# What GpSimd waits for before its indirect transfers: landings, or TensorE's counts

## The reference, cut to what matters

```python
# x: (8, 512, 256) f32; 32 experts, 6 of them per token
xn = layernorm(x)
s = attention_over_channels(xn)         # per batch: softmax over a 256x256 matrix of channels
for e in range(32):                     # combine: softmax gate, 3 of 8 groups, top 6, normalized
    y += combine[:, e] * ((silu(xn @ w1[e].T) * (xn @ w3[e].T)) @ w2[e].T)
shared = (silu(xn @ sw1.T) * (xn @ sw3.T)) @ sw2.T
out = x + s * silu(y + shared)
```

## Time and profile before

| | |
|---|---|
| median of 3 runs | 969.05 us (965.66 to 969.32) |
| profiled execution, its own time | 964.12 us |
| its span | 962.4 us |
| PE / DVE / POOL / ACT busy | 596.8 / 506.7 / 399.2 / 341.5 us |
| mean granted clock of PE | 0.804 |
| DMA moved | 174.75 MB, mean 182 GB/s |

### The profile page before, as it was taken

How to read it: one execution, slowest core, us unless ns; L and a number is a source line. 1 busy time by engine, 2 the same in 40 slices (tenths; PEclk the granted TensorE clock), 3 DMA queues, 4 the chain that set the end, 5 groups by cost and what they waited for, 6 DMA issues and landing times.

```text
span 962.4 us, 13698 instructions
## 1 busy us (share of the span) xinstructions
PE 596.8 (62%) x3728; PEld 486.4 (51%) x3728; DVE 506.7 (53%) x1412; ACT 341.5 (35%) x684; POOL 399.2 (41%) x401
## 2 busy tenths in 40 slices
PE   5788782928375776001979776758486765658540
PEld 4567551817164654001968665546375654547430
DVE  7877863736374771000535555546465645646543
ACT  3343431332323242001646443435254443435330
POOL 0135345455364663663001444343444444453443
PEclk9798795867768686655979797879799897979875
DMA  9994572634524223224437675758677675848552
GB/s 335 390 356 164 182 262 93 234 132 140 210 73 141 76 93 132 82 82 136 145 120 218 192 237 171 219 154 251 176 220 224 189 208 168 241 148 259 164 170 76
DMA packets 134232, 174.75 MB, mean 182 GB/s; under 512 B 12433, under 2 KB 120722, under 8 KB 133266
## 3 DMA queue, kind: packets, MB, share of 16 engines
q1 hardware_dynamic: 109698, 107.77, 34.3%
q0 software_dynamic: 18432, 50.36, 17.4%
q10 hardware_dynamic: 6032, 15.76, 4.7%
HBM read 81.56 MB, written 92.28 MB: 181 GB/s over the span
## 4 chain that ended last, share of the span: by engine, by line
DMA 57%; issue 21%; POOL 9%; PE 8%; DVE 4%; POOLq 1%; ACT 0%; SPq 0%; DVEq 0%; ACTq 0%
DMA early<-slots_d,slot_at 30%; DMA slots_d<-early,slot_at 23%; POOL slots_d L391 7%; PE ps L696 4%; DMA slots_d<-pad 3%; DVE ps L957 3%; POOL early L408 2%; PE ps L715 2%; PE ps L684 1%; PE ps L706 1%; DVE work L974 1%; POOLq L391 0%; SPq L290 0%; DMA work<-slots_d 0%; DMA slots_d<-early 0%
## 5 line engine op out<-in xcount | busy, mean ns | idle before, releaser
L408 POOL DMA_INDIRECT early<-slots_d,slot_at x192 | 191.7, 999 | 316.9 <-DVE ps L957 108.2
L391 POOL DMA_INDIRECT slots_d<-early,slot_at x192 | 205.4, 1070 | 237.8 <-DMA slots_d<-early,slot_at 170.5
L696 PE MATMUL ps<-w_all,work 128*128 x1344 | 186.5, 294 | 57.3 <-issue 54.2
L696 PEld LDWEIGHTS ps<-w_all,work 128*128 128x128 f16 x1344 | 140.5, 105 | 83.1 <-issue 60.4
L684 PE MATMUL ps<-ident,work 128*128 128x128 f32 x448 | 75.2, 294 | 140.1 <-DMA work<-slots_d 65.9
L957 DVE SCALAR_TENSOR_TENSOR ps<-early,wk,ps 128x256 f32<-128x256 f32 x160 | 77.8, 486 | 116.9 <-DMA early<-slots_d,slot_at 115.5
L684 PEld LDWEIGHTS ps<-ident,work 128*128 128x128 f32 x448 | 54.7, 151 | 155.7 <-issue 81.4
L974 DVE SCALAR_TENSOR_TENSOR work<-ps,work 128x512 f16<-128x512 f32 x112 | 76.8, 686 | 103.6 <-ACT work L517 102.1
L517 ACT ACTIVATE work<-ps 128x512 f16<-128x512 f32 x112 | 66.6, 595 | 141.0 <-PE ps L684 128.1
L715 PE MATMUL ps<-w_all,work 128*128 x672 | 99.9, 289 | 2.5 <-DVE work L987 2.0
L524 ACT ACTIVATE work<-ps 128x256 f32<-128x256 f32 x112 | 43.0, 384 | 157.1 <-PE ps L696 127.4
(11 more groups left out here) (140 smaller groups left out, 811.6 us busy)
## 6 DMA issues: line engine op xcount, KB each, us to landing
work<-slots_d SPq DMA_DIRECT2D x112, 256.0 KB
slots_d<-early SPq DMA_DIRECT2D x112, 256.0 KB
slots_d<-pad SPq DMA_DIRECT2D x7, 3072.0 KB, 15.5
w_all<-in_wexp ACTq DMA_DIRECT2D x7, 1536.0 KB, 6.9
slots_d<-pad SPq DMA_DIRECT2D x1, 7168.0 KB, 30.0
s_all<-in_x SPq DMA_DIRECT2D x8, 512.0 KB, 4.8
ysh_d<-work ACTq DMA_DIRECT2D x8, 512.0 KB
early<-ysh_d SPq DMA_DIRECT2D x32, 128.0 KB
```

Source lines behind the costliest of these rows:

```text
L391: pool.indirect_dma_start(slots_d[:, :], bass.IndirectOffsetOnAxis(ap=slot_at[:, at:at + 1], axis=0), xn[b % XN_RING][:, t, :], None, boun ...
L408: pool.indirect_dma_start(gath[:, at % RING, :], None, slots_d[:, :], bass.IndirectOffsetOnAxis(ap=slot_at[:, at:at + 1], axis=0), bounds_ ...
L696: mm = pe.matmul(ps[:, 2 + p % 2, h * 2 * I:(h + 1) * 2 * I], xT[p % 2][:, x_low, h, k, :], w16[:, bass.ds(at_weights[2 * p + h] + w_low * ...
```

## The change

GpSimd no longer waits for the landing of its own transfers. In stage 1 every second scatter waits for a count that PE raises: the function `let_pass` gives for scatter n of batch b the semaphore and the value, in the order in which PE reaches them, from the turn of batch b+1 to the first product of batch b+1's attention. The last batch has six such waits, the last of them for PE's last count of the stage. In stage 2 a gather of pair q (two per pair) waits for PE's hidden matmuls of pair q+21 if it is even, and for PE's transposes of pair q+20 if it is odd, both capped at the last pair; the waits for stores and for the ring stay. The scatters' semaphores are three now, one per `xn` buffer, and all who wait for scatters wait on these. SP waits for batches 2 and 5 alone before it loads the last weights.

```diff
-FLIGHT = 2
@@ semaphores
-        s_disp = sems("s_disp", FLIGHT)
+        s_disp = sems("s_disp", XN_RING)
@@ SP
-            for f in range(FLIGHT):
-                sp.wait_ge(s_disp[f], 16 * (BATCH_ROWS // FLIGHT) * (B - 2))
+            sp.wait_ge(s_disp[2], 16 * BATCH_ROWS * 2)
...
-            for f in range(FLIGHT):
-                sp.wait_ge(s_disp[f], 16 * (BATCH_ROWS // FLIGHT) * B)
+            for k, n in enumerate((3, 3, 2)):
+                sp.wait_ge(s_disp[k], 16 * BATCH_ROWS * n)
@@ GpSimd
+            def let_pass(b, n):
+
+                nxt = b + 1 < B
+                due = {4: (s_s_ps, b + 1), 8: (s_y_ps, 2 * b + 1), 10: (s_r_ps, b + 1), 12: (s_y_ps, 2 * b + 2),
+                       14: (s_m_ps, b + 1), 18: (s_at_ps, 2 * b + 2)}
+                if nxt:
+                    due.update({2: (s_xt_ps, 2 * b + 4), 6: (s_lg_ps, b + 2), 16: (s_cnt, b + 2),
+                                20: (s_ab_ps, HC * b + HC + 1), 22: (s_a_ps, b + 2)})
+                if n in due:
+                    pool.wait_ge(*due[n])
+
...
-                        if at >= FLIGHT:
-                            pool.wait_ge(s_disp[at % FLIGHT], 16 * (at // FLIGHT))
+                        let_pass(b, t * TOP_K + k)
...
-                                                oob_is_err=False).then_inc(s_disp[at % FLIGHT], 16)
+                                                oob_is_err=False).then_inc(s_disp[b % XN_RING], 16)
...
-                    if at >= FLIGHT:
-                        pool.wait_ge(s_gath[(at - FLIGHT) % RING], 16 * ((at - FLIGHT) // RING) + 16)
+                    ahead = at // 2 + 21
+                    if at % 2 == 0:
+                        pool.wait_ge(s_eab_ps, min(ahead + 1, PAIRS))
+                    else:
+                        pool.wait_ge(s_ehT_ps, min(ahead, PAIRS))
@@ DVE, normal(b)
-                    for f in range(FLIGHT):
-                        dve.wait_ge(s_disp[f], 16 * (BATCH_ROWS // FLIGHT) * (b - XN_RING + 1))
+                    dve.wait_ge(s_disp[b % XN_RING], 16 * BATCH_ROWS * (b // XN_RING))
```

## The result

The changed kernel takes **813.48 us** (median of 4 executions, 805.62 to 827.74), the kernel before beside it 967.99. Two of the four executions (819.64 and 827.74) fell in a slower state and are left out of the ratio, which is 0.8333, 95% interval 0.8299 to 0.8368; the other two took 805.62 and 807.32. The forecast was 765 with a range of 745 to 820. The profiled execution took 805.62 us for a span of 803.8. Of the 158.6 us by which the span fell, 117.2 came before the expert stage starts; the rest came in that stage, 473.3 us long where it had been 514.7, and forecast were 434.5.

The account below looks back on a forecast made before the run. Bound by latency of GpSimd's indirect DMA transfers and waits for their landing, not traffic. Terms 327.1 + 87.7 + 311.5 + 35.3 = 761.6 span, 763.3 for the execution, 766 with run offset, stated as 765; range 745 to 820.

Parts of the forecast that it names:

- Rival 1: Stage 2: store and gather each land 3 us later, using up the slack; a dozen takes 48.4, total 792; chance 0.17.
- Rival 2: Both stages: indirect transfers are served one after the other, 1.59 us per scatter; stage 2 +64, 829; chance 0.12.
- Rival 4: Stage 1 keeps half its wait because GpSimd, released in bursts, falls behind; 795 us; chance 0.06.
- (a): Stage 1: scatters released by TensorE's counts end line 755's landing wait, batches every 37.57 us; 60.9 us saved.
- (b): End of stage 1: the last expert weights wait for batch 5 alone and come 5.6 us earlier.
- (c): Scatter tail after TensorE's stage 1 work: stage 2 starts at 327.1 instead of 447.67, 120.6 us earlier in all.
- Start to pair 24: Beginning of stage 2, from its first slot load to pair 24: as before, 87.7 us.
- (d): Stage 2: gathers released by TensorE's counts, dozens of 43.4 us; seven 311.5 with 1.1 each for crowded DMA, 63.8 saved.
- (e): End of stage 2, from pair 108 on: 35.3 us instead of 51.75, 16.4 saved.
- the slack of 4.9 us: Stage 2: sum 0's gathers and sums need 17.5 us of the 22.4 between pair 18 and pair 26.
- Rival 3: Stage 2 release loop: gathers wait on TensorE, TensorE on sums, sums on gathers; slower, 970 and more; chance 0.03.
- my 315: Stage 2: DMA engines move 315 GB/s at most, 2.9 us per pair, adding up to 1.1 us a dozen.

Follow-up runs that it names:

- g1: The kernel before with the change's gathers only, scatters still waiting for landings; 86.0 us saved, stage 2 takes 429.0 us.
- c1: The changed kernel without the scatters' waits for TensorE's counts (`let_pass` left out); a batch takes 44.0 us, total not given.
- f3: b1 with a waited write of 1024 columns on GpSimd after every second gather; 820 us.
- b1: The changed kernel with its gathers waiting for no count of TensorE, only for the ring's free place and the stores; 858 us.
- d1: The changed kernel with each gather fetching 64 of 256 columns, a quarter of the bytes; a dozen takes 49.3 us, total not given.

## Why the prediction was right, and what it missed

The sign and the two mechanisms held. The size held with luck: 813.48 lies in the range of 745 to 820, but outside the forecast's own 748 to 785, and in it only by the room made for rivals 1, 2 and 4, none of which was what happened. The profiled span was forecast at 761.6 and is 803.8; term by term, 42.2 us:

- **(a), (b), (c), stage 1: 3.4 us short.** The period is 37.5 as forecast, and the landing waits at the refill went. Scatters had fallen behind their counts at the end: the last 15 ran back to back, and the last started at 327.96, against 324.6 forecast (6.5 and 2.5 make 326.9 and not the 327.1 that I wrote; the landing in that row is 2.55). Rival 4 (half of the wait kept) fell. On chips I and II it would have been 12 to 16 us short; "remote" waits stand in stage 1 there, and in this profile too (line 490, 37.7 us).
- **Start to pair 24:** 87.2, forecast 87.7.
- **(d), the dozens: the term that failed, 36.1 of the 42.2.** "The sums stop waiting" held: 7.4 us left. "So a dozen costs 43.4" didn't follow here, because I took it that a count is there when TensorE is done, and it was late 55 times. Where counts aren't late, it does follow: g1 has dozens of 43.5, with the register loads bare (7.7 and 8.4 us of idle time at two of them) as I had put it, and the whole stage takes 429.0 where I had 434.5. The 1.1 us that I added for crowded queues weren't needed.
- **(e), the tail:** 38.5 instead of 35.3; g1 has 36.7.
- The median lies 7.9 above the profiled execution, where I had allowed 2. The four executions spread over 22 us; the twelve kernels of the experiments spread over 1 to 12, with and without late counts, so what set the two long ones apart isn't known.

**The rivals.** Rival 1 came nearest in the length of a dozen (48.4, and 49.6 measured), for the wrong reason: the sums hardly wait for a landing, so the slack of 4.9 us held. Rival 2 fell: transfers overlap, 15 scatters went out at 1.28 us each to the end and the last landed within 2.6 us of its start. Rival 3, the loop, would show as sums waiting for gathers, and doesn't. What the list lacked was a cost of the burst itself: before, runs of gathers are of one or two, and I read their harmlessness as a property of the transfers and not of the spacing.

**Where DMA could bind.** g1's stretches, with two columns at the end, DMA share and GB/s:

```profile
721.00:726.00 5.00, 4.86 (x45) 4.25 (x43) 4.44 (x11) 3.32 (x8) 2.17 (x3) 1.00 1.00 321
726.00:731.00 5.00, 4.85 (x45) 4.22 (x43) 4.77 (x12) 3.60 (x8) 2.99 (x3) 1.00 0.99 298
```

The engines are full at 321 GB/s, near my 315 and short of the 358 that the Trainium skill, DMA: Bandwidth & Descriptors, Specifications, gives. TensorE's pairs go on meanwhile: from 716.31 to 742.23 nine take 2.88 us each, 0.26 over the quiet 2.62. So full queues can have cost 2.6 us a dozen at most, with VectorE's sums in the same 0.26.

**Do the parts add up?** The scatters alone saved 105.5 us (chip I), the gathers alone 86.0 (chip III), both together 161.5 by the two executions of the ratio (154.5 by the median). The 30 us between are near what the dozens lost in the changed kernel (36.1) and g1's did not, but the three figures come from different chips, and stage 1 alone differs by some 10 us among them. By forecast the parts were 120.6 and 80.2.

## What to carry to other kernels

Before you take away the landing waits between an engine's indirect transfers, note that they also space the transfers; put something in their place (here counts that TensorE reaches anyway), and look for the place where several such waits are met at once and a burst goes out all the same. After such a change read ScalarE's and VectorE's idle time behind TensorE: a start well after TensorE's end, or a wait for a "remote" in a program of one core, was the sign of late counts here. Before you spend time on them, run the same kernel on a second chip and look whether its trace lacks records of counts: on one chip of three nothing was late, and no spacer was needed. And where a spacer is put in, work out the queue's own period first: 1.94 us a gather was already too slow for this kernel, 1.62 on average was not.

## What the runs showed of the hardware

- In recorded executions TensorE's counts came up to 5.2 us late (6.4 in the place of c1's stage 1 above) while GpSimd started indirect transfers 1.28 to 1.30 us apart, and then together; ScalarE's and VectorE's counts didn't. In runs of two of f3 they were at most 1.2 late, in b1's runs of six 5.2; fewer bytes (d1) changed nothing. Two chips of three did this, and the one of the changed kernel's profile; their traces, and the one of the kernel before, also lack 8 to 15% of the records of TensorE's counts in stage 2.
- An indirect transfer mostly costs GpSimd 0.97 to 1.00 us (mean 1.01 for the gathers) and 0.30 to the next. With a waited write of 64 columns between them it is 0.94 to the next: 0.17 for the write and 0.77 behind it.
- The same instructions of the first part took 328 to 331 or 339 to 343 us by chip, while the kernel before, whose landings space its transfers, took 962 to 970.
